# Denominators spread on chip, reciprocals five steps earlier, and one queue's transfers in another order

## What is computed

```python
x = x + tanh(g_xattn) * xattn(layernorm(x), ctx_2048)   # 8 heads of 16, softmax over 512 keys
x = x + tanh(g_ffn) * ffn(layernorm(x))                 # rmsnorm, 8 experts, top 2, and a shared one

def xattn(x1, x2):                      # x1, x2: (batch, 128, 512), channels first
    q, k, v = proj(x1, Wq, bq), proj(x2, Wk, bk), proj(x2, Wv, bv)
    attn = softmax(einsum('bhqd,bhkd->bhqk', q, k) / sqrt(16), axis=-1)
    out = einsum('bhqk,bhkd->bhqd', attn, v)
```

## Time and profile before

| | |
|---|---|
| median of 3 runs | 1444.71 us (1438.89 to 1447.31) |
| the profiled execution, its own time | 1441.5 us |
| its span, first to last instruction | 1439.6 us |
| mean granted TensorE clock | 0.974 |
| busy: TensorE, VectorE, ScalarE, GpSimd | 93%, 68%, 61%, 60% |

### The profile page before, as it was taken

How to read it: one execution, slowest core, us unless ns; L and a number is a source line. 1 busy time by engine, 2 the same in 40 slices (tenths; PEclk the granted TensorE clock), 3 DMA queues, 4 the chain that set the end, 5 groups by cost and what they waited for, 6 DMA issues and landing times.

```text
span 1439.6 us, 24599 instructions
## 1 busy us (share of the span) xinstructions
PE 1339.7 (93%) x7290; PEld 648.5 (45%) x7290; DVE 974.5 (68%) x1661; ACT 872.5 (61%) x1720; POOL 867.6 (60%) x1278
## 2 busy tenths in 40 slices
PE   2899999999999989998989999989999999999997
PEld 1222222222222222232222222267778888888886
DVE  5888788988788878897878888656654333333332
ACT  2588787877777767786767777734333433333332
POOL 7447667767776777677767864633212555555553
PEclk7799999999999999999999999999999999999999
DMA  6566666666767666766666766276653788785655
GB/s 177 160 190 206 191 202 198 195 199 185 188 178 181 197 183 174 187 199 181 180 182 185 188 160 172 92 206 138 150 183 82 188 215 205 182 198 110 111 110 81
DMA packets 161308, 247.90 MB, mean 172 GB/s; under 512 B 33605, under 2 KB 58828, under 8 KB 161182
## 3 DMA queue, kind: packets, MB, share of 16 engines
q1 hardware_dynamic: 142926, 208.96, 51.6%
q0 software_dynamic: 18256, 37.38, 14.0%
HBM read 141.85 MB, written 103.88 MB: 171 GB/s over the span
## 4 chain that ended last, share of the span: by engine, by line
PE 34%; DMA 21%; SPq 12%; issue 11%; DVE 9%; POOL 8%; ACT 4%; POOLq 1%; ACTq 0%; DVEq 0%
PE m_banks L949 17%; DMA parts_k<-arena 11%; SPq L470 8%; DMA arena<-pv_d 6%; DVE row_max L1122 6%; PE bank L906 4%; PE bank L877 4%; PE m_banks L856 3%; PE bank L837 3%; SPq L456 3%; POOL xs L780 2%; DMA out<-xs,ids 2%; POOL arena L679 2%; POOL arena L676 2%; POOL arena L677 2%
## 5 line engine op out<-in xcount | busy, mean ns | idle before, releaser
L1122 DVE TENSOR_REDUCE row_max<-m_banks 128x2 f32<-128x1024 f32 x512 | 614.4, 1220 | 82.1 <-PE m_banks L856 77.5
L1394 ACT ACTIVATE arena<-bank 128x512 f32<-128x512 f32 x1024 | 556.6, 606 | 127.8 <-PE bank L877 124.8
L877 PE MATMUL bank<-arena 112*128 112x512 bf16 x1024 | 317.7, 389 | 6.0 <-ACT arena L1394 1.8
L906 PE MATMUL bank<-arena 128*32 128x512 f32 x2048 | 278.9, 617 | 0.3 <-ACT arena L1401 0.3
L792 POOL DMA_INDIRECT out<-xs,ids x71 | 112.5, 1584 | 173.6 <-ACT xs L1468 138.4
L856 PE MATMUL m_banks<-arena 48*128 48x512 bf16 x1024 | 169.7, 395 | 27.0 <-DVE row_max L1122 20.7
L877 PEld LDWEIGHTS bank<-arena 112*128 112x128 bf16 x1024 | 79.7, 100 | 255.5 <-ACT arena L1394 91.6
L949 PE MATMUL m_banks<-w_ring,h_hi 128*128 x568 | 183.1, 403 | 0.0
L1457 ACT ACTIVATE arena<-m_banks 128x256 f32<-128x256 f32 x103 | 39.5, 384 | 190.4 <-PE m_banks L949 190.3
L676 POOL TENSOR_TENSOR arena<-arena 128x512 bf16<-128x512 f32 x62 | 71.6, 1156 | 110.3 <-ACT arena L1386 107.4
L856 PEld LDWEIGHTS m_banks<-arena 48*128 48x128 bf16 x1024 | 39.7, 94 | 164.1 <-issue 81.9
(11 more groups left out here) (176 smaller groups left out, 2037.9 us busy)
## 6 DMA issues: line engine op xcount, KB each, us to landing
pv_d<-arena SPq DMA_DIRECT2D x32, 512.0 KB, 4.3
w_ring<-split_d SPq DMA_DIRECT2D x60, 256.0 KB
parts_k<-arena SPq DMA_DIRECT2D x96, 128.0 KB
parts_q<-arena SPq DMA_DIRECT2D x96, 128.0 KB
arena<-parts_k SPq DMA_DIRECT2D x64, 192.0 KB, 3.7
arena<-parts_q SPq DMA_DIRECT2D x64, 192.0 KB, 3.8
arena<-in_w SPq DMA_DIRECT2D x36, 256.0 KB, 7.0
arena<-in_ctx SPq DMA_DIRECT2D x32, 256.0 KB, 3.4
```

Source lines behind the costliest of these rows:

```text
L877: nc.tensor.matmul(out, k_stack[b % 3][0:SHIFTED, h, kt * P:(kt + 1) * P], q_stack[b % 3][0:SHIFTED, h, :], start=True, stop=True).then_in ...
L906: last = nc.tensor.matmul(pv_ps[2 * DH * j:2 * DH * (j + 1), :], v_ones[b % 3][:, kt, GROUP * g + j, :], probs[pair % 3][:, j, :], start=( ...
L1122: nc.vector.reduce_max(pair, m_ps[(STEPS * b + u) // 2 % M_PAIRS], AX_X).then_inc(s_mx, 1)
L1394: nc.scalar.activation(probs[group % 3][:, j, :], bank_of["scores", b, s], ACT.Exp, scale=float(DH) ** -0.5).then_inc(s_exp, 1)
```

## The change

`load_denominators` goes. In its place `spread_denominators` copies the denominators of each half g straight from `pv_sb` on four partitions (512 values each) to 64 partitions of `den_c` (32 values each), by two transfers within on-chip memory, issued ahead of `store_values`. Their semaphore counts twice as many increments. `invert` moves from step 16 to step 11. `store_reciprocals` takes the place that `load_denominators` had. `load_values`, which now also waits for the store of pv_sb, moves ahead of the reads of the q parts. `take_values` waits in addition for the spread of the entry before.

```diff
-RECIP_AT = 16
+RECIP_AT = 11
-            def load_denominators(b):
-                sp.wait_ge(s_w, DMA * (b + 1))
+            def spread_denominators(b):
+                sp.wait_ge(s_u, 2 * b + 2)
                 if b:
                     sp.wait_ge(s_rc, b)
-                sp.dma_start(den_c, pv_d[:, DH, :].rearrange("h (c w) -> h c w", c=DH)).then_inc(s_sc, DMA)
+                for g in range(2):
+                    sp.dma_start(den_c[P // 2 * g:P // 2 * (g + 1), :], pv_sb[DH:P:2 * DH, g, :]).then_inc(s_sc, DMA)
...
             def load_values(b):
                 sp.wait_ge(s_r, DMA * (b + 1))
+                sp.wait_ge(s_w, DMA * (b + 1))
...
                 if is_b(i - 1):
+                    spread_denominators(i - 1)
                     store_values(i - 1)
                 if is_b(i + 2):
                     read(i + 2, 0)
                     write(i + 2, 1, MID)
                     write(i + 2, 1, LO)
                 if is_b(i - 1):
-                    load_denominators(i - 1)
+                    store_reciprocals(i - 1)
                 if is_b(i + 4) and i + 4 >= 2:
                     load_ctx(i + 4)
                 if is_b(i - 3):
                     store_turned(i - 3)
                 if is_b(i - 1):
-                    store_reciprocals(i - 1)
+                    load_values(i - 1)
                 if is_b(i + 2):
                     read(i + 2, 1)
                 if is_b(i + 1):
                     row(i + 1, 0)
-                if is_b(i - 1):
-                    load_values(i - 1)
...
                 if j == 0:
+                    spread_denominators(B - 1)
                     store_values(B - 1)
                 if j == 1:
                     store_turned(B - 3)
-                    load_denominators(B - 1)
...
             def invert(b):
-                dve.wait_ge(s_sc, DMA * (b + 1))
+                dve.wait_ge(s_sc, 2 * DMA * (b + 1))
...
                 if b:
                     act_e.wait_ge(s_w, DMA * b)
+                    act_e.wait_ge(s_sc, 2 * DMA * b)
                 nc.scalar.copy(pv_sb[:, g, :], pv_ps).then_inc(s_u, 1)
```

## The result

The changed kernel takes 1495.8 us (median of 6 runs, 1485.65 to 1500.72), the kernel before 1445.96 us beside it: a ratio of 1.034, 95% interval 1.030 to 1.038. It is slower by 3.4%, on the side of the forecast's slower rival and outside its range.

The account below looks back on a forecast made before the run. TensorE's own work was taken as the bound of a turn. 42.9 - 9 - 10 = 24 us, plus one outside the window, gives 25 off 1441.5: 1416.5, forecast as 1419 us on the runs' scale, range 1402 to 1432.

Parts of the forecast that it names:

- slower rival: SP's queue: load_values' 512 KB in front makes the maxima rows land late, 2.3 us a turn, about 1461 us; chance 0.10.
- The bound and the stall: TensorE's turn: own work bounds it at 26.54 us; late denominators cause the L865 wait, 31.6 us in 19 turns.
- The denominators' path: Spreads to step 11: no wait in early turns; TensorE loses 0.7 us in 13 late turns, 9 us.
- The early turn: Turn whose k parts land early: second spread lands at +5.6 us, before step 11 at +6.7, so no wait.
- late turns: Turns whose k parts land late: denominators land at +8.5 to +10.5 us, TensorE loses 0 to 3.3 us.
- The feared 43 us for spreads on four engines: Denominators' path: if each spread stays on four engines, 13 x 3.3 = 43 us in place of 9.
- what is late next: Rows of the maxima, needed at step 0: landing of 5 us, TensorE loses 0.8 us in 13 turns, 10 us.
- the bound of 42.9 us: 26 turns, 1.65 us each above TensorE's own work: the most that a change to waits there can give.
- The relief of the burst: 512 KB leave the burst before the k writes, 2.6 us at 201 GB/s; k writes land sooner, partly offsetting late rows.

Follow-up runs that it names:

- both cures: The changed kernel with load_values put back behind the rows of the maxima and all scatters moved behind the turns; ratio 0.994 (0.992 to 0.997) to the kernel before.

## Why the prediction was wrong

**The bound and the stall.** Right. With both cures the turns come to 26.7 us beside the 26.5 of the bound. The wait at L865 came from the denominators, and all of it went (31.6 us to nothing, first halves of 13.0 us).

**The denominators' path.** The early turn was right (landing by +6.7). The price for late turns, 13 x 0.7 = 9 us, was not paid in the kernel after: no late turn is left, since the k parts land sooner once 512 KB leave the burst. Where load_values was put back late turns exist, and VectorE stands 15 us in 8 of them; what of that reaches TensorE isn't shown. The feared 43 us for spreads on four engines did not come, L1115 has no wait in any turn. But that price was for late turns too, so it doesn't show how many engines a spread uses.

**The step that failed** is "what is late next": "I take a landing of 5 us, the middle of the two, which gives 0.5 to 1.6 us late, and count 0.8", 10 us in all, for 13 turns. The second row landed after 8.4 us in the turn shown, and after up to 10.9 in others, among the landings that the view resolves. TensorE stood 63.4 us, in 24 turns. The rows went out about when forecast: SP came to them at +17.7 to +19.4 in turns 2 to 29, so the second was issued by about +20.0. It was the landing that was mis-sized. The lower end of that range was a landing with short queues at the start of a turn, which is not what stands in the queue at its end. The place had its own row, 7.3 us, and the prediction itself moved 512 KB in front of it. The arithmetic for that stood in the slower rival (7.6 us, 2.3 us a turn; measured 2.5) and got a chance of 0.10, on the ground that the queue can drain while SP issues the q reads. It doesn't: between 340 and 800 us the reads of the parts (L470) land after up to 8.9 us, where 4.3 was the longest before.

**Luck in that rival.** Its 2.3 us a turn come from the 512 KB alone. Where these meet no scatters, the wait is much smaller: 7.1 us in turns 2 to 9, and 16.3 us in 29 turns with the scatters behind the turns, where the rows landed after 5.9 us at most (of the landings that the view resolves). So the rival named the right wait and one of its two causes, and its size agrees by accident. By the same token the forecast's 5 us of landing and 10 us of waiting are not far from what the queue does without scatters.

**The scatters** don't occur in the prediction at all. They are GpSimd's, not SP's, and nothing in the diff touches them. But the landing of 7.3 us is from a turn that has them, and the turns of the kernel before are longer from turn 10 on too (28.2 us against 27.1).

**What was left out of every case** is the clock. The prediction read it in the earlier trace rows as a part of the old loss and priced no new stall with it. From turn 2 to the last mark the stretch grew by 52 us. TensorE's named waits went up by 41 us (47.7 to 88.7) and its busy time by 13 us (758.1 to 771.2), small gaps making up the difference. With both cures, on another chip and at a clock of 1.00, the same work has a busy time of 743.8 us. So the old clock loss of 14 us, which the bound of 42.9 us counted as gone, became one of 27. That is most of what lies between the rival's 1461 us and the measured 1496.

**The relief of the burst** was counted at a part of 0.8 us and was larger: it alone removes the stall that the change set out from (the kernel before with only the order changed).

## What to carry to other kernels

When a transfer is moved ahead on a queue, price the transfers behind it by their own landing at that place and not by the landing of the same line at a quieter time, and price what a stall does to the clock with it. Then look for what lands there just in time before the change: a wait of 1 us that shows once, as the one for these rows did, may be the next limit of the loop. Ask too what other engines' queues carry at that moment: here small transfers that the change doesn't touch turned a wait of 0.9 us a turn into one of 2.8. A change that does two things against one stall should be tried by halves; here one half was worth 1.8% and the other cost all of it and more.

## What the runs showed of the hardware

- The row copies of 4 KB each, SBUF to SBUF, took 1.7 to 10.9 us to land between 340 and 800 us of the kernel after, among those that the view resolves; their size was the same each time, what stood in the queues was not.
- Two loads of 256 KB in head-by-head patterns, one of them reading each row sixteen times, made TensorE wait nearly twice as long for the transfers behind them as two loads of 128 contiguous rows of 2 KB (66.8 to 73.7 us against 37.0).
- Two scatters of 128 elements of 8 bytes in a turn of 27 us, from another engine's queue, are worth 5% of this kernel beside full queues (1.032 to 0.982), and they cost in each of the three places tried.
- On-chip spreads from four partitions to 64 landed in time in every turn of the kernel after; in the turn shown the reciprocals ran about 3.9 us behind the issue of the second spread.
- Stalls of TensorE shorter than 3 us were followed by a granted clock under 1.00 in some turns and not in others: 0.88 behind 1.56 us and 1.00 behind 2.09 us in the kernel before, 0.92 behind 1.77 us and 1.00 behind 2.46 us in the kernel after.
- A burst of 64 scatters behind the turns, where there had been 16, cost the jobs there 23 us in one kernel and 56 us in another, of 525; in the second it went with a stretch of 50 us in which TensorE was busy for 13.4.
